# A gated cross-attention block with a top-2 mixture of experts: the last dispatch group, the first looped tiles and the final sums in another order

## The reference

```python
x = x + jnp.tanh(g_xattn[0]) * _L0_xattn_ref(ctx_1024, ctx_1024, _layernorm(x), ...)   # x, ctx: (16, 64, 128) float32
x = x + jnp.tanh(g_ffn[0]) * _L0_ffn_ref(_layernorm(x), ...)

# _L0_ffn_ref: 8 experts, top 2, D = 128, F = 512
probs = jax.nn.softmax(jnp.einsum('bsd,ed->bse', x, gate_w), axis=-1)
topk_probs, topk_idx = jax.lax.top_k(probs, 2)
oh = jax.nn.one_hot(topk_idx, 8)
h = jax.nn.gelu(jnp.einsum('bsd,fed,bske->bskf', x, w1, oh) + jnp.take(b1, topk_idx, axis=0))
y = jnp.einsum('bskf,def,bske->bskd', h, w2, oh) + jnp.take(b2, topk_idx, axis=0)
out = jnp.sum(y * topk_probs[..., None], axis=-2)
```

## Time and profile before

| what | us |
|---|---|
| median of 3 runs | 98.57 (98.53 to 100.66) |
| the profiled execution | 98.16 |
| its span from first to last instruction | 96.4 |
| PE, PEld, DVE busy | 77.2, 66.7, 69.1 |
| ACT, POOL busy | 55.6, 49.7 |

### The profile page before, as it was taken

How to read it: one execution, slowest core, us unless ns; L and a number is a source line. 1 busy time by engine, 2 the same in 40 slices (tenths; PEclk the granted TensorE clock), 3 DMA queues, 4 the chain that set the end, 5 groups by cost and what they waited for, 6 DMA issues and landing times.

```text
span 96.4 us, 2735 instructions
## 1 busy us (share of the span) xinstructions
PE 77.2 (80%) x828; PEld 66.7 (69%) x828; DVE 69.1 (72%) x313; ACT 55.6 (58%) x170; POOL 49.7 (52%) x81
## 2 busy tenths in 40 slices
PE   4968997676857438898848399999999999999930
PEld 1355665364654326898837299999999999999930
DVE  2179729998979899999859865659978755324970
ACT  4185599897996594533652744765765765741000
POOL 6965499006777777760000487754745646205600
PEclk9999999996555555899999999999999999999999
DMA  2999997950121111352055455521001011086015
GB/s 24 302 401 428 428 428 313 308 164 12 43 62 55 55 55 55 115 154 73 0 125 121 113 147 133 132 73 53 27 14 46 8 43 31 17 231 211 0 53 164
DMA packets 11630, 12.58 MB, mean 130 GB/s; under 512 B 1363, under 2 KB 10599, under 8 KB 11360
## 3 DMA queue, kind: packets, MB, share of 16 engines
q1 hardware_dynamic: 10384, 10.01, 32.5%
q0 software_dynamic: 1088, 2.05, 6.6%
q10 hardware_dynamic: 144, 0.35, 1.5%
HBM read 8.18 MB, written 4.42 MB: 131 GB/s over the span
## 4 chain that ended last, share of the span: by engine, by line
PE 39%; DVE 29%; DMA 10%; issue 5%; SPq 4%; ACT 4%; POOL 3%; DVEq 1%; POOLq 0%
PE bank L807 18%; DMA dispatched<-pad_rows 5%; PE bank L791 4%; PE bank L793 4%; PE bank L792 4%; DMA wp<-in_wpack 4%; SPq L328 3%; PE bank L774 2%; DMA in_rows<-dispatched 2%; POOL rstd L411 2%; DVE x L941 2%; PE bank L684 2%; DVE xn L877 2%; DVE stats L948 1%; DVE hot L917 1%
## 5 line engine op out<-in xcount | busy, mean ns | idle before, releaser
L598 ACT ACTIVATE hid<-bank,wp 128x128 f32<-128x128 f32 x92 | 26.3, 368 | 21.1 <-PE bank L793 21.1
L459 POOL DMA_INDIRECT results<-y_sb,in_rows x18 | 18.0, 1000 | 21.6 <-DVE y_sb L1111 11.4
L807 PE MATMUL bank<-w_sb,hid 128*128 (+1 forms) x184 | 25.7, 282 | 0.9 <-ACT hid L598 0.9
L807 PEld LDWEIGHTS bank<-w_sb,hid 128*128 128x128 f32 x184 | 22.3, 192 | 1.4 <-ACT hid L598 1.4
L374 POOL DMA_INDIRECT dispatched<-rows,slot x16 | 15.8, 990 | 9.9 <-DVE slot L1012 6.0
L791 PE MATMUL bank<-xs_t,w_hi 128*128 128x128 f16 x76 | 13.7, 219 | 0.6 <-DVE w_lo L1030 0.4
L792 PE MATMUL bank<-xs_t,w_hi 128*128 128x128 f16 x76 | 13.7, 219 | 0.0
L793 PE MATMUL bank<-xs_t,w_lo 128*128 128x128 f16 x76 | 13.7, 219 | 0.0
L1105 DVE COPY xs_t<-bank 128x256 f16<-128x256 f16 x19 | 5.5, 291 | 4.5 <-PE bank L774 4.3
L791 PEld LDWEIGHTS bank<-xs_t,w_hi 128*128 (+1 forms) x76 | 7.5, 98 | 0.9 <-issue 0.9
L792 PEld LDWEIGHTS bank<-xs_t,w_hi 128*128 (+1 forms) x76 | 7.4, 98 | 0.2
(11 more groups left out here) (176 smaller groups left out, 180.7 us busy)
## 6 DMA issues: line engine op xcount, KB each, us to landing
w_sb<-in_w SPq DMA_DIRECT2D x2, 2048.0 KB, 11.1
in_rows<-dispatched SPq DMA_DIRECT2D x23, 65.0 KB, 1.9
results<-zeros SPq DMA_DIRECT2D x1, 1024.0 KB, 4.9
res<-results SPq DMA_DIRECT2D x4, 256.0 KB, 3.7
dispatched<-pad_rows SPq DMA_DIRECT2D x9, 65.0 KB, 4.6
ctx_sb<-in_ctx_t SPq DMA_DIRECT2D x1, 512.0 KB, 5.3
out<-out_sb SPq DMA_DIRECT2D x4, 128.0 KB, 2.0
wp<-in_wpack ACTq DMA_DIRECT2D x1, 342.0 KB, 3.6
```

What stands on the lines that cost most here:

```text
L459: pool.indirect_dma_start(results_dram, bass.IndirectOffsetOnAxis(ap=in_rows[:].bitcast(U32)[:, t, TARGET:TARGET + 1], axis=0), y_sb[:, t, ...
L598: mm = act.activation(hid[:, t % HIDS, b, :], hid_ps[t % HID_PS][:, b * P:(b + 1) * P], ACT.Gelu_apprx_tanh, bias=b1[:, experts[t], b:b + ...
L807: mm = pe.matmul(to, hid[:, t % HIDS, b, :], w2_sb[:, e, b * P:(b + 1) * P], start=False, stop=b == BLOCKS - 1)
```

## The change

- **Last group.** In `places` the positions of the early experts come from `chosen` and the ranks directly. For the last group, gates and slots follow the places at once, then the counts, four of expert 0's eight comparisons, the pad addresses, and then the row splits of groups 2 and 3 with the other comparisons. PE's first gather waits for each group's low halves by itself.
- **Set-up.** `lanes` runs after the fill instead of between the choice and the norm of group 1, `bias_high` before the last group's rows, and GpSimd's 1024-column iota behind its second result scatter. The table steps stand behind the comparisons of all four experts.
- **Hidden units** go to four half-used PSUM banks instead of three full ones, with semaphores for each half of a tile, so that GELU and output can begin on two blocks.
- **Main loop.** PE runs hidden(t), output(t-1), turn_rows(t+2), sum_last(t-2). VectorE makes the low weights 5, 6 and 7 between the tiles, and ScalarE multiplies by the first four gates, one behind the GELUs of each of the tiles 5 to 8. The sums of chunks 0 and 2 are one tile earlier. `sum_last` takes all first halves, then all second ones.
- **Stores** of chunks 1 and 3 are issued by ScalarE.

```diff
-HID_PS, HIDS, XS = 3, 3, 3
+HALVES, HIDS, XS = 2, 3, 3
-        gather_ps = [bank[4], bank[7]]
+        gather_ps = [bank[4], bank[0]]
-        hid_ps = [bank[1], bank[5], bank[3]]
+        hid_ps = [bank[1], bank[5], bank[3], bank[7]]
 # GpSimd
-            pool.iota(token_i[:], [[1, TOKENS]], base=0, channel_multiplier=0).then_inc(tokens_set, 1)
...
                                         oob_is_err=False).then_inc(scattered, 16)
+                if t == 1:
+                    pool.iota(token_i[:], [[1, TOKENS]], base=0, channel_multiplier=0).then_inc(tokens_set, 1)
 # ScalarE
+            def first_gated(t):
+                act.wait_ge(loaded[t], 16)
+                act.wait_ge(first_out_ok, t + 1)
+                act.activation(y_sb[:, t, :], y_sb[:, t, :], ACT.Copy, scale=in_f[:, t, GATE:GATE + 1]).then_inc(gated_ok, 1)
...
-                act.wait_ge(hid_in_ps, t + 1)
                 for b in range(BLOCKS):
+                    h = HALVES * t + b // HALVES
+                    if b % HALVES == 0:
+                        act.wait_ge(hid_in_ps, h + 1)
...
+                    if b % HALVES == HALVES - 1:
+                        mm.then_inc(hid_ok, 1)
...
+                if EARLY + 1 <= t < 2 * EARLY + 1:
+                    first_gated(t - EARLY - 1)
+            for i, q in list(enumerate(chunks))[1::2]:
+                act.wait_ge(out_ok, i + 1)
+                act.dma_start(out_view[:, q, :], out_sb[:, q, :]).then_inc(stored, 16)
 # PE
-                    pe.wait_ge(low_ok, GROUPS)
...
+                    if e == 0 and t in STARTS:
+                        pe.wait_ge(low_ok, STARTS.index(t) + 1)
 # PE, output(t)
-                pe.wait_ge(hid_ok, t + 1)
                 for b in range(BLOCKS):
+                    if b % HALVES == 0:
+                        pe.wait_ge(hid_ok, HALVES * t + b // HALVES + 1)
 # PE, main loop
-            output(EARLY - 1, experts[EARLY - 1])
-            for t in range(EARLY, N_TILES + LAG + 1):
+            for t in range(EARLY, N_TILES + 2):
                 if t < N_TILES:
                     hidden(t, experts[t])
-                if t + LAG < N_TILES:
-                    turn_rows(t + LAG)
...
-                if EARLY + LAG <= t < N_TILES + LAG:
-                    output(t - LAG, experts[t - LAG])
-                if t - LAG - 1 >= SCATTERED:
-                    sum_last(t - LAG - 1)
+                if t <= N_TILES:
+                    output(t - 1, experts[t - 1])
+                if t + LAG < N_TILES:
+                    turn_rows(t + LAG)
+                if t - 2 >= SCATTERED:
+                    sum_last(t - 2)
 # VectorE, last group
                     places(g)
-                    rows_low(g)
-                    one_hots(0)
                     gates(g)
                     slots(g)
+                    counted()
+                    one_hots(0, 0, STARTS[2])
+                    pads()
+                    rows_low(2)
+                    one_hots(0, STARTS[2], STARTS[3])
+                    rows_low(3)
+                    one_hots(0, STARTS[3])
 # VectorE, loaded tiles
-            weights_lo(w1_lo, w1_sb, w1_hi, w1hi_ok, w1_ok, EARLY + 1)
             split_rows(EARLY + LAG)
-            for i in range(EARLY + 2, PARTS):
-                weights_lo(w1_lo, w1_sb, w1_hi, w1hi_ok, w1_ok, i)
-            for t in range(EARLY):
-                first_gated(t)
+            low_weights(5)
-            for t in range(EARLY, N_TILES + LAG):
+            for t in range(EARLY, N_TILES + 1):
                 if t + LAG < N_TILES:
                     copy_rows(t + LAG)
                 if t + LAG + 1 < N_TILES:
                     split_rows(t + LAG + 1)
+                if t + 2 in (6, 7):
+                    low_weights(t + 2)
-                if t >= EARLY + LAG:
-                    gated(t - LAG)
+                if t - 1 >= EARLY:
+                    gated(t - 1)
+                if t == N_TILES - 2:
+                    summed = [base_sum(DVE_CHUNKS[0])]
+                if t == N_TILES - 1:
+                    summed.append(base_sum(DVE_CHUNKS[1]))
```

More of the change, by code:

```diff
@@ L363, in _ @@
                 sp.dma_start(res[:, q, :, :], res_view[:, q, :, :]).then_inc(ld_res[i], 16)
[L364 removed]
+            for i, q in list(enumerate(chunks))[0::2]:
                 sp.wait_ge(out_ok, i + 1)
@@ L815, in sum_last @@
                     pe.wait_ge(xs_ok, N_TILES - EARLY)
-                for h in range(2):
-                    for j in range(HALF):
-                        to = sum_ps[h][:, j * P:(j + 1) * P]
-                        at = whose[:, i, (h * HALF + j) * P:(h * HALF + j + 1) * P]
-                        pe.matmul(to, at, y_16[:, i, 0, :], start=i == 0 and j == 0, stop=False)
-                        mm = pe.matmul(to, at, y_16[:, i, 1, :], start=False, stop=i == LAST - 1 and j == HALF - 1)
-                    if i == LAST - 1:
-                        mm.then_inc(last_ps[h], 1)
+                for c in range(2):
+                    pe.wait_ge(y16_ok, 2 * i + c + 1)
+                    for h in range(2):
+                        for j in range(HALF):
+                            to = sum_ps[h][:, j * P:(j + 1) * P]
+                            at = whose[:, i, (h * HALF + j) * P:(h * HALF + j + 1) * P]
+                            mm = pe.matmul(to, at, y_16[:, i, c, :], start=i == 0 and j == 0 and c == 0, stop=i == LAST - 1 and j == HALF - 1 and c == 1)
+                        if i == LAST - 1 and c == 1:
+                            mm.then_inc(last_ps[h], 1)
             experts = [slice(e, e + 1) for e in range(EXPERTS)]
@@ L911, in _, with one_hots @@
             pos_made = {}
-            def one_hots(e):
+            def one_hots(e, a=0, b=TILES):
                 v.wait_ge(dve, pos_made[GROUPS - 1])
-                for t in range(TILES):
+                v.wait_ge(numbers_set, 6)
+                for t in range(a, b):
                     v.tensor_scalar(hot[:, e, t, :], slot_no[:], float(FIRST_ROW + e * REGION), pos[:, t, e:e + 1],
@@ L1032, in _ @@
             for step, g in ORDER:
-                if step == NUMBERS:
-                    lanes()
-                elif step == MAXIMUM:
+                if step == MAXIMUM:
                     score_max(g)
```

108 lines of the change are left out of this document (51 added, 57 removed).

## The result

| | median of its executions, us | median of the kernel before beside it | ratio with 95% interval |
|---|---|---|---|
| changed kernel, first four | 94.54 (93.88 to 95.77) | 98.62 | 0.957 [0.947, 0.967] |
| changed kernel, six more (r1_same) | 94.45 | 99.79 | 0.960 [0.948, 0.971] |

The change is faster by about 4.1 us, where 2.8 were forecast. Some executions of either kernel fall into a slower state, which the medians include and the ratios leave out; without them the first four have a median of 94.06, under the range's low end of 94.5. The sign and most of the places were right, the size was not.

The account below looks back on a forecast made before the run. PE was taken to bound the steady part at 1.78 us a tile, with losses between 47 and 57 us. 1.22 + 2.05 - 0.55 + 0.1 = 2.8 us off the median 98.57 gave 95.7, range 94.5 to 97.4.

Parts of the forecast that it names:

- Step 7: GpSimd's scatters with the iota moved behind the second: last ends near 77 plus one, read-back at 82.8, no cost.
- step 2: Split of tile 4 waits for VectorE instead of the reads, starting near 47.95 instead of 49.23: gain 1.28 us.
- Step 1: Start of the reads: last group's places at 34.42, pad addresses at 36.24, about 1.5 us earlier, first read at 45.9.
- Step 3: Hidden(4) starts at 49.35 instead of 51.57, output(3) remains behind it: net gain 1.22 us; the halves' gather-loop gain worth nothing.
- Step 4: PE's waits between 51.57 and 56.46: moving low weights and first gates out of the way gains 2.05 us, 0.5 left lost.
- Step 5: ScalarE's new gate multiplications and half-tile semaphores fit its 0.64 us of idle time in each tile: cost nothing.
- Step 6: End of the loop: `sum_last` must wait for the last tile's transposes to be copied out: loss 0.55 us, once.
- Step 8: Tail: second store queue gains 0.2 us, first sums released 0.2 later, PE's 0.1 wait goes: gain together 0.1.
- The reads start no earlier: Rival at the reads: the last send may hold SyncE, split of tile 4 stays at 49.23; 97.0 us, chance 0.15.
- The clock did come up later: Rival in the first gather: the clock rises 3 us later, PE loses some 0.6 us; 96.3 us, chance 0.10.
- The slower rival: Clock stays at 1.2 GHz through all four gathers, hidden(4) at 55.6 instead of 49.35; 102.0 us, chance 0.04.
- the late scatters: Rival at the end: ScalarE's gates 2 us later, read-back at about 84.8, last sums wait; 96.7 us, chance 0.10.

Follow-up runs that it names:

- e13_before_parked: The kernel before with only GpSimd's iota moved, released by low weight 4 (the fifth); 98.46 us, ratio 0.988.
- r2_lanes: The changed kernel with `lanes` back between the choice and the norm of group 1; 94.55 us, ratio 0.958.
- r4_full: The changed kernel with hidden units in three full PSUM banks and one semaphore for each tile instead of each half; 94.97 us, ratio 0.967.
- e10_stores: The changed kernel with all four stores on SyncE, as before; 94.32 us, ratio 0.960.
- e12_iota_parked: The changed kernel with the first `sum_last` behind hidden(21) and GpSimd's iota released by low weight 3 (the fourth); 93.62 us, ratio 0.950.
- e7_weights: The changed kernel with low weights 5 to 7 and the four first gates back on VectorE ahead of the loop; 94.92 us, ratio 0.964.
- e9_order: The changed kernel with PE's main loop in the old order, VectorE's results and sums one tile later, and an added wait before hidden; 95.80 us, ratio 0.973.
- r5_sum: The changed kernel with the first `sum_last` moved behind hidden(21); 93.73 us, ratio 0.952.
- e8_iota_twice: The kernel before with GpSimd's iota run twice in a row in front; 100.06 us, ratio 1.019.
- b_same: The kernel before, unchanged, run once more; 99.04 us, ratio 1.002.
- r6_sum: The changed kernel with the first `sum_last` behind hidden(21), run a second time; 94.27 us, ratio 0.957.
- e5: The changed kernel with GpSimd's iota put back in front, between the two memsets; 94.91 us, ratio 0.961.
- e6: The kernel before with GpSimd's iota alone moved behind the second result scatter; 99.81 us, ratio 1.011.

## Why the prediction was wrong in size

- **The failed step is 7**, with a second term in step 2. Step 7 took up the iota's move, and costed it only where it went to. Where it came from, it had held VectorE on the path to the last group: 0.92 for a row of 0.17 at 15.84. That is 4.39 - 3.86 = 0.53 of the front, shown by e13_before_parked. The prediction quoted the iota's row for its length, and didn't set VectorE's rows of the same time beside it. The Trainium skill (SBUF — State Buffer, "SBUF: two separate sides") says that VectorE and GpSimd share one pair of ports under an exclusive lock: GpSimd's instruction and a VectorE instruction in a two-port mode fully block each other, one with two SBUF inputs only against a GpSimd instruction that reads SBUF. By that rule an iota, which reads nothing, blocks the TENSOR_SCALAR and the cast, if they are in such a mode, and lets the TENSOR_TENSOR rows pass, but an addition of GpSimd's doesn't let VectorE's additions pass. The traces agree: 0.92, 0.64, 1.43 and 1.76 for the first kind, 0.15 and 0.29 for the second, and 0.97 for 0.42 where two additions meet.
- **Step 1, the front.** Places at 34.42 forecast, 33.77 measured: 0.65 earlier, 0.53 from the iota and 0.17 since this execution's first statistics came at 14.87 instead of 15.04, less 0.05. `lanes` gave the 0.36 that was counted (0.37 in r2_lanes). Pad addresses at 35.46 (forecast 36.24), 0.8 earlier, nearly all of it from the places. The first read, forecast at 45.9, came at 44.43 here, 3.56 behind the start of the last send, and at 46.74 in the first profile.
- **Step 2, the first split bound by VectorE.** The mechanism is right, its length isn't. It came at 46.81, with no DMA wait: 1.14 earlier than forecast, 0.65 of it from the front. The other 0.49 is the length of the stretch from the places to the split: it took 13.04, and I had 47.95 - 34.42 = 13.53, the old length with `lanes` added (the rows give 47.92 - 34.78 = 13.14 and 0.36, so 0.03 was rounding). I took the same instructions in another order to take the same time. By the distances from start to start, `lanes` took 0.34, and the table's steps took 2.82 instead of 3.06, gates, slots, counts and pad addresses 0.79 instead of 0.90, and each of three groups, the 32 comparisons, the low half of the bias and the four low weights, 0.08 less; a wait of 0.15 for the exponentials went the other way. No run tests this term by itself.
- **Step 3.** Hidden(4) at 48.29 (forecast 49.35), with output(3) behind it: right. Its sentence that the halves are "worth nothing" was wrong once the front was earlier: hidden(3)'s last matmuls are at 47.5, and tile 4's split is done at 47.35. PE and VectorE now arrive together, and without halves PE is 0.84 later (r4_full). In r1_same PE comes last by 0.2: from the split to hidden(4) lie 1.48, against 1.27 and 1.28 in e10_stores and e12_iota_parked, where the clock rose at 39.81 and 39.02.
- **Step 4.** Its total held: PE's waits of 3.5 us between 47 and 58 went to none, and the three longer periods behind hidden(4) (1.95, 1.92 and 1.80 against 1.785) cost 0.3 of the 0.5 that I had left, 0.16 of it the iota's. Its cause was only partly right. Spreading the low weights and moving the gates is worth 0.5 to 0.7 (e7_weights). The new order in PE's loop, which I had costed only for output(3), is worth 1.6 in the profile of e9_order together with the hold that it hides (0.88) and a wait that only that kernel has (0.41); its ratio, 1.3% above that of r1_same, isn't clear of the intervals.
- **Step 5.** ScalarE's extra work costs nothing: the gates took 0.40, and PE waits for no GELU from 47 to 88.
- **Step 6.** -0.55 forecast, 0.59 measured (r5_sum: 44.09 to 43.50).
- **Step 7, the scatters.** Last scatter at 76.86 (forecast 77), first read-back used at 82.90 (82.8): right. The 0.16 in the cast that meets the iota I had at nothing.
- **Step 8.** Forecast 0.1, measured 0: from the last matmul to the end 4.10 before and after. The second store queue gives 0.2 (e10_stores), and the first sums start 0.03 behind the last matmul instead of 0.19 ahead of it, which takes it.

Together: 1.06 of the missing 1.2 us lies ahead of hidden(4) (0.65 + 0.49, less 0.08 by which the way from the split to hidden(4) took longer), 0.16 behind it.

**The rivals.** "The reads start no earlier" came about in part in the first profile: VectorE waited 0.58 for the rows and split at 48.51. The clock did come up later, at 40.77 and 42.02 in the two profiles against 39.32, but hidden(0) and the gathers ran through it, and PE arrived 0.2 behind VectorE. It isn't a consequence of the change: in profiles of the kernel before and its variants the clock rose anywhere from 39.32 to 41.6. The slower rival and the late scatters didn't appear.

**What stays open.** Parts of the change undone one at a time sum to less than 4.1 us, since PE's gather loop and VectorE's work end within 0.2 of each other and each hides the other's loss. The positions from `chosen`, the new place of `bias_high` and that of the table's first steps weren't undone by themselves. Of e8_iota_twice's 1.9% the profile shows 0.6 us.

## What to carry to other kernels

When an instruction of GpSimd moves, read VectorE's rows at both its old and its new time: one that takes several times its usual length and ends with GpSimd's is a term of the sum. Put such an instruction where VectorE has only work that isn't held, and check by the row. And when two engines reach a point together, a term costed at nothing because the other was later must be costed again with every gain that is found ahead of it.

## What the runs showed of the hardware

- GpSimd's 1024-column iota (0.99 us) held VectorE's TENSOR_SCALAR (128x2, SBUF to SBUF) until its end, 0.92 and 0.64 for 0.17, and not TENSOR_TENSOR, TENSOR_REDUCE or SCALAR_TENSOR_TENSOR rows that ran beside it in e8_iota_twice and e12_iota_parked.
- GpSimd's addition of 128x256 fp32 values in SBUF (0.73 us) does hold VectorE's of the same form: VectorE's took 0.97 in b_same and 0.96 in r1_same beside it, and 0.42 without.
- A 128x128 cast from fp32 to fp16 that began during an indirect DMA's instruction, right ahead of an iota, was held through both: 1.43 and 1.76 for 0.22. Beside scatters alone no cast took over 0.46.
- The half-clock stretch lies differently from execution to execution of one kernel: 20.29 to 40.77 and 21.54 to 42.02 in the changed one. It lasted 17.07 us in three of the 18 profiles (before, e10_stores, e12_iota_parked) and 20.48 in the others. Where the gather loop sets hidden(4), a later rise moves it: PE's last matmul of hidden(3) starts at 46.68, 47.58 and 48.00 with rises at 39.02, 40.77 and 41.70 (e12_iota_parked, r1_same, r6_sum). A second one of 3.4 us, from 7.5 to 7.9 on, stood in four profiles (one of the changed kernel, e5, e6, e9); in these four VectorE's first statistics came at 15.69 to 15.89, in the others at 14.74 to 15.29.
